# A graph network on one core: the last 190 scatters by source wait for the last product of the first build

## The reference, cut to what matters

```python
edge_index = jnp.stack([src, dst])
h = jnp.maximum(_layernorm(x, axis=-1), 0.0)
x = x + _L0_gnn_ref(h, edge_index, ...)         # attention over edges, 4 heads
h = jnp.maximum(_layernorm(x, axis=-1), 0.0)
x = x + _L1_gnn_ref(h, edge_attr_20, ...)       # messages x[col] * filter(edge), summed by row
h = jnp.maximum(_layernorm(x, axis=-1), 0.0)
x = x + _L2_gnn_ref(h, src, dst, edge_weight, edge_weight_n2, ...)   # weighted sums both ways, gate
h = jnp.maximum(_layernorm(x, axis=-1), 0.0)
x = x + _L3_gnn_ref(h, edge_index, ...)         # two attentions of one head, and an MLP
```

```python
filt = jax.nn.silu(rbf @ Wf1 + bf1) @ Wf2 + bf2
msg = x[col] * filt
agg = jax.ops.segment_sum(msg, row, num_segments=x.shape[0])
```

## Time and profile before

| | us |
|---|---|
| median of 3 runs | 7822.07 (7807.66 to 7825.48) |
| the profiled execution, its own time | 7872.61 |
| its span in the trace | 7870.9 |

### The profile page before, as it was taken

The page is one execution under the profiler, slowest core; times in us unless marked ns, Lnnn a source line. Parts: engine busy times, 40 slices in busy tenths (PEclk is TensorE's granted clock), DMA queues, the critical chain, the costliest instruction groups (busy, mean ns, idle before and its releaser), DMA issues.

```text
span 7870.9 us, 88068 instructions
## 1 busy us (share of the span) xinstructions
PE 5294.4 (67%) x23224; PEld 3511.6 (45%) x23225; DVE 4742.8 (60%) x6614; ACT 2203.1 (28%) x4590; POOL 2850.9 (36%) x4180
## 2 busy tenths in 40 slices
PE   8523444699944448883388866666666799994838
PEld 4312233487822126763233325555555645483213
DVE  9862222475521127879999987777777610026987
ACT  6411111243311115522255541112211310012524
POOL 0277777517767771000000005666676000000000
PEclk9995666799955559996699987777777799995968
DMA  9940111259976663336422325656566223304775
GB/s 253 274 106 11 37 39 40 73 167 292 292 234 215 211 213 134 129 107 175 134 67 67 83 72 187 194 193 197 195 201 189 45 97 132 132 30 123 205 195 150
DMA packets 717764, 1158.60 MB, mean 147 GB/s; under 512 B 273349, under 2 KB 487003, under 8 KB 702994
## 3 DMA queue, kind: packets, MB, share of 16 engines
q1 hardware_dynamic: 374010, 608.16, 26.7%
q10 hardware_dynamic: 228664, 291.39, 11.1%
q0 software_dynamic: 114784, 255.38, 10.2%
HBM read 670.62 MB, written 483.97 MB: 147 GB/s over the span
## 4 chain that ended last, share of the span: by engine, by line
PE 34%; DVE 28%; issue 17%; DMA 9%; another core or an unknown queue 8%; POOL 2%; ACT 1%; SPq 1%; DVEq 1%; ACTq 0%; POOLq 0%
PE psall L1497 10%; PE psall L1470 7%; DVE arena L2167 7%; DVE arena L2135 4%; PE psall L1563 3%; DMA arena<-weights_out 3%; PE psall L1630 3%; DMA arena<-weights_in 2%; DVE arena L2362 2%; DVE arena L2219 2%; DVE arena L2160 2%; DMA arena<-table_x,arena 2%; POOL arena L959 2%; PE psall L1575 1%
## 5 line engine op out<-in xcount | busy, mean ns | idle before, releaser
L959 POOL DMA_INDIRECT arena<-table_x,arena x856 | 955.5, 1116 | 2182.1 <-DMA arena<-slots_by_src 1849.8
L1497 PE MATMUL psall<-arena 128*128 128x250 f32 x2880 | 864.1, 447 | 468.3 <-issue 426.0
L1540 PE MATMUL psall<-arena 128*65 128x312 f32 (+3 forms) x3000 | 948.5, 440 | 217.8 <-DVE arena L2167 217.6
L1470 PE MATMUL psall<-shared_w,arena 128*128 128x256 f32 x3264 | 855.2, 419 | 308.2 <-DVE arena L2079 279.0
L923 POOL DMA_INDIRECT slots_by_block_pair<-arena x806 | 797.9, 990 | 562.1 <-DVE arena L1944 314.5
L1116 ACT ACTIVATE arena<-psall 128x250 f32<-128x250 f32 (+2 forms) x1002 | 327.0, 367 | 2145.5 <-PE psall L1497 767.0
L1497 PEld LDWEIGHTS psall<-arena 128*128 128x128 f32 x2880 | 581.1, 217 | 751.8 <-issue 700.0
L948 POOL DMA_INDIRECT slots_by_src<-arena,pos_s x806 | 783.0, 971 | 268.6 <-issue 171.8
L1470 PEld LDWEIGHTS psall<-shared_w,arena 128*128 128x128 f32 x3264 | 664.2, 210 | 427.9 <-DVE arena L2079 271.7
L1563 PE MATMUL psall<-arena 128*125 128x256 f32 x1712 | 585.5, 515 | 345.5 <-DVE arena L2219 241.4
L2079 DVE TENSOR_TENSOR arena<-psall,shared_w 128x512 f32<-128x512 f32 x408 | 280.2, 690 | 820.0 <-remote 510.8
(11 more groups left out here) (323 smaller groups left out, 7496.6 us busy)
## 6 DMA issues: line engine op xcount, KB each, us to landing
arena<-counts SPq DMA_DIRECT2D x375, 312.5 KB, 3.4
arena<-slots_by_src SPq DMA_DIRECT2D x107, 1040.0 KB
filters<-arena ACTq DMA_DIRECT2D x204, 520.0 KB
slots_by_src<-shared_on SPq DMA_DIRECT2D x8, 9230.0 KB
arena<-filters SPq DMA_DIRECT2D x138, 520.0 KB
counts<-arena ACTq DMA_DIRECT2D x125, 312.5 KB
weights_in<-arena ACTq DMA_DIRECT2D x125, 312.5 KB
arena<-counts ACTq DMA_DIRECT2D x25, 1562.5 KB
```

The source lines that it names most:

```text
L959: G.indirect_dma_start(hg[:, f % 2, j, :], None, t_x1, bass.IndirectOffsetOnAxis(ap=pay_s[:, f % 2, j, S_IDX:S_IDX + 1].bitcast(I32), axis ...
L1470: last = MM(to, hidT[:, sl % 2, c, j * LANES:(j + 1) * LANES], wf2[:, c, :], start=(c == 0), stop=(c == 1))
L1497: MM(psall[:, bass.ds(half_at(words[k], j), 2 * P)], ohs[:, sl, TG * k + j, :], ohw[:, sl, TG * k + j, :, :].rearrange("p a k -> p (a k)") ...
L1540: last = MM(ps[gat_bank(n, wn, h_, c)][0:F + 1, 0:z - a], rows, g["e1"][:, q % RE, a:z], start=(b == 0), stop=(b == NT - 1))
```

## The change

One constant and one wait are added. `S2_G` is 202 and `SLOTS` is 4, so `S2_LATE` is group 154, and the scatters from there on are 806 - 616 = 190 (the constant's 12 x 4 groups of four would be 192; the last group has two).

```diff
@@ -82,6 +82,8 @@
 
 S2_EARLY = 16 * SLOTS
 assert S2_EARLY <= 4 * NT + 7 - SLOTS
+
+S2_LATE = S2_G - 12 * SLOTS
 
 
 def skewed(eng, turns, slots, stages, tail=0):
@@ -944,6 +946,9 @@
                     pool.wait_ge(ringed[g % SLOTS], 16 * (1 + (ring_count(g - SLOTS) if g >= SLOTS else 0)))
                 else:
                     pool.wait_ge(fst[g % SLOTS], 16 * (FILTERS + (g - S2_EARLY) // SLOTS + 1))
+                if g == S2_LATE:
+
+                    pool.wait_ge(s["cb_mm"], 1 + T1)
                 for c in range(TG * g, min(TG * (g + 1), EC)):
                     G.indirect_dma_start(slots_s, bass.IndirectOffsetOnAxis(ap=pos_s[:, c:c + 1], axis=0),
                                          ring_s[:, g % SLOTS, c % TG, :], None).then_inc(ringed[g % SLOTS], 16)
```

## The result

The changed kernel takes **7720.7 us** (median of 4 runs, 7703.2 to 7726.7) where the kernel before takes 7818.9 us (4 runs, 7807.7 to 7825.5). The ratio is 0.9876, with a 95% interval of 0.986 to 0.9893: 98 us less. The prediction said 7703 us, 119 less; 119 lies just outside that interval, which ends at 109. The profiled execution has a span of 7724.9 us, and before it was 7870.9.

The account below looks back on a forecast made before the run. The build was taken as bound by PE's queue beside POOL's scatters. Build 214 us earlier, maxima ending at 3674, 83 us of remaining scatters and 15 more start the attention at 3772, 119 earlier: 7703 us, range 7620 to 7790.

Parts of the forecast that it names:

- The build: First build, from 2705 us: 2385 MATMULs at 0.2452 us without scatters, last product at 3290 instead of 3504, 214 us earlier.
- the prediction's last part: Signs in the trace: 2385 build MATMULs from 2705 to 3290, clock 1.00, POOL idle; scatters about 3.15 us beside maxima.
- Rival 5: First build stays slow without scatters, last product still at 3504, attention 95 us later: 7917 us; chance 0.03.
- One scatter for each maximum: Beside the maxima POOL gets one turn per border of two DVE instructions: 100 scatters instead of one per 1.41 us.
- Rival 1: Maxima don't hold POOL: all 190 scatters at 1.41 us, done in 268 us, DMA decides; 7637 us, chance 0.17.
- rival 2: POOL gets no turn between maxima: 159 scatters follow them, attention 11 us later than before; 7833 us, chance 0.09.
- 0.11 us of DVE for each border: Cost to DVE of each scatter slipping in beside the 100 maxima, which would take 360 us instead of 349.
- Rival 3: A scatter holds DVE for its whole length, 0.97 us; maxima take 446 us; 7789 us, chance 0.11 with its half case.
- The start of the maxima: Maxima begin 24 us after the build's last product, at 3314 us, with 17 scatters issued.
- SP's queue: SP's ring loads delay the attention until 176 scatters are through; 59 remain after the maxima, 83 us with DVE idle.
- The filters don't suffer so: Filters beside scatters keep their pace, unlike the build: 525 MATMULs in 100 us beside scatters, 529 without.
- Rival 4: The maxima's transposes stall on PE beside scatters as the products did: 186 us lost, 7794 us; chance 0.03.

Follow-up runs that it names:

- group A: Follow-up runs on one chip, the same as group C's, where the kernel before took 7848 us; the kernel before, unedited and traced again, took 7854.5 us.
- group C: Follow-up runs on group A's chip; against the kernel before at 7745.3 us, POOL loading the whole ring took 7226.4 us, the changed kernel once more 7599.8 us.
- groups B and D: Follow-up runs on two other chips, called the fast chips, each with its own runs of the kernel before, which took 6891 and 6878 us there.

## Why the prediction was right

**The build.** Predicted to end 214 us earlier, at 3290; it ended 219 us earlier, at 3284, at the rate taken from the fast part of the same loop. The granted clock, the idle POOL and the number of MATMULs are as the prediction's last part asked. Rival 5 (slow without scatters) is out. The median of 355 ns for a register operation, which the prediction read from 2800 to 2900, is that of a stretch with 38 of them; from 2300 to 2700 the median is 18 and the longest 1405. So PE's queue is held by a few long operations among many short ones. This changes no term of the sum, which goes by the rate of the MATMULs.

**One scatter for each maximum.** Right, and with it the sum: 259 instructions of POOL (a scatter and a memset each) in 390 us. A scatter took 3.01 us (predicted 3.15), and 100 of them started beside the maxima. Rival 1 had 0.97 us, rival 2 scatters of a hundred us; both are out.

**0.11 us of DVE for each border.** This is the term that was mis-sized: it was 11 us, and the maxima took 348 us, no longer than before. The prediction took it from one CAST behind one scatter; beside maxima, and beside the attention's instructions too, DVE gives nothing. Rival 3, with a whole scatter's length, is further off still. The Trainium skill, page "SBUF — State Buffer", section "SBUF: two separate sides" with its part "Who interferes with whom", bears on this: a DVE instruction with two inputs in SBUF contends with POOL's reads, which agrees with the scatter of 3.01 us. By the same section the one of the two that starts first has the pair for its whole instruction and the other "fully blocks"; this doesn't show on DVE's side, where the maximum that starts inside a scatter (at 3400.51, the scatter from 3398.30 to 3401.31) takes 3.41 us as any other.

**The start of the maxima.** Predicted 24 us after the last product, as before; it was 36. ACT was 17.9 us at issuing its two loads of counts beside the scatters, 10.5 before, and its first mask came 8.4 us behind them instead of 4.9. The prediction took no harm: more scatters get through meanwhile, as it said (25 instead of 17 ahead of the first maximum).

**SP's queue.** The step that distinguishes the prediction from "they stand beside the maxima for nothing": DVE idle behind the last maximum for 83 us of scatters, 98 in all with the terms. Measured 93 us from the last maximum to the attention, and with the loads given to POOL they went to 21. Two parts differ from the forecast, and that they work against each other is luck. Only 51 of the 176 scatters were left instead of 59, 72 us instead of 83, since 25 and not 17 had gone ahead of the maxima; and the way from SP's store to the attention took 16.5 us beside scatters (3745.5 to 3762.0) instead of 12.1. The last maximum ended at 3669 instead of 3674 (5 from the build and 12 from DVE's borders, less 12 from their later start). So the attention started 129 us earlier (predicted 119). DMA had a share of 0.84 from 3310 to 3700 (predicted 0.84 beside the maxima) and cost the maxima nothing.

**From the trace to the time.** The attention's start moved 10 us more than forecast and the time 21 less (98 instead of 119), so that the forecast of the time is the weaker part. The spans differ by 146 us: 129 up to the attention and 17 behind it, which is spread. The profiled execution of before was 54 us above the median of its four runs, and that of after 6; 146 - 54 + 6 = 98. That is bookkeeping: the prediction took the 50 us that it knew of as lying where the change doesn't act, and said itself that up to 15 us of gain might go missing if they lay in the slow build. No run locates them. Against the second trace of the kernel before (group A, attention at 3879.5) the start moves by 117 us.

**What the prediction read too narrowly.** "The filters don't suffer so" was taken from 1900 to 2000 us alone. Between 700 and 900 the filters suffer as much, on this chip: 264 MATMULs where the fast chip makes 1057, though by SP's queue and not by PE's. The stretch that was quoted is the one in which POOL loads the ring itself. The contrast between these two, which the trace of before already had, pointed to a version (POOL loads the whole ring) that gains three and a half times what the change does (519 us against 146 in group C). It changes no term of the sum. Rival 4 (transposes held as the products were) leaned on it; they were in fact not held (627 MATMULs of PE between 3310 and 3700, at the granted clock of before, 0.61).

## What to carry to other kernels

Before moving work out of a slow stretch, compare the stretches in which the same work stands beside the same engine and does no harm: here the ring's load after each fourth scatter, issued by the engine that scatters and not by SP, was there in the fast stretch and absent in the slow one, and extending it gave 7226 us of 7745 (on the fast chip 6669 of 6891), where the wait gave 7600. When transfers wait for work that you delay, read what stands behind them in the issuing queue: a ring's loads ahead of the next stage's first load cost 70 us in the changed kernel and 222 on the fast chip. Time such a change on more than one chip: the wait, which pays where the queue is held, gave nothing on a fast chip in its version with 126 late scatters (ratio 0.9997). And when two stages are slow beside the same work, read each engine's queue operations in both before taking them for one effect: here it was PE's queue in one and SP's in the other.

## What the runs showed of the hardware

- **A queue held by another engine's scatters, on one chip of three.** Beside unbroken indirect scatters 1.41 us apart, PE's queue takes up to 1421 ns for a register operation of 37 ns, in the first comparison and in groups A and C (one chip). On the two chips of groups B and D it never does (42 ns at most in every build traced there), and the kernel before is there 11 to 12% faster. It is not always PE's queue: beside the first sort's scatters PE's register operations take 32 to 36 ns and SP's a median of 465 (37 on the fast chip). SP's issues of two loads of edge attributes then stand 2.4 us apart, and 0.6 on the fast chip (timelines of SP's queue, the kernel before and the one with the loop written out):

```profile
802.00 0.01 SPq L724 DMA_DIRECT2D arena<-in_edge_attr  x1
804.44 0.01 SPq L725 DMA_DIRECT2D arena<-in_edge_attr  x1
```

```profile
800.19 0.43 SPq L724 DMA_DIRECT2D arena<-in_edge_attr  x1
800.80 0.63 SPq L725 DMA_DIRECT2D arena<-in_edge_attr  x1
```

- **What frees it is not settled.** With POOL's own load after each fourth scatter and none by SP it is free; with plain transfers in the scatters' place it is free; with a quarter of PE's increments it is held as before. The filters don't part the two conditions that are left: SP loads no ring there, but it does issue its loads of edge attributes beside the scatters. The run that was to part them came to a chip without the effect, and so did the one with the loop written out. Why the chips differ is open too (three chips, and only the slow one seen more than once), and so is whether the first sort's scatters, beside which the filters lose some 600 us on the slow chip (the build starts at 2187 there and at 1562 on the fast one), could be broken up in the same way.
- **POOL and DVE.** A scatter that meets DVE instructions with two SBUF inputs in a row gets through at each border and costs DVE nothing: 3.01 us beside maxima of 3.41, up to 1.70 beside the attention's of 0.80 and 0.86 (417 of 418 scatters), with DVE's pace unchanged in both (3.46 us from maximum to maximum; 268 instructions in 200 us of attention, 267 without scatters).
